# Perceiver block on one core: tile 1's attention and projection ahead of tile 0's FFN, four rotating x buffers, scale rows and half of Wo's low parts on GpSimd

## The reference

```python
# fq(x, s, z) = (clip(round(x / s + z), 0, 255) - z) * s ; ln = layer norm without weights
x = x + fq(ln(x)) @ fq(ctx)                      # x: 16 x 64 x 1024, ctx: 16 x 1024 x 1024
qkv = ln(x) @ Wqkv                               # 32 query heads of 32, one K and one V head
x = x + softmax(q k^T / sqrt(32) + alibi, causal) v @ Wo
routing = softmax(ln(x) @ gate_w.T)              # 8 experts
in_s, out_s = routing @ in_channel_scale, routing @ out_channel_scale
x = x + (ln(x) * in_s) @ sign(W).T * out_s + bias
```

## Time and profile before

| | us |
|---|---|
| median of 3 runs (454.27 to 456.82) | 455.64 |
| the profiled execution's own time | 456.7 |
| its span, first to last instruction | 454.9 |

### The profile page before, as it was taken

The page is one execution under the profiler, slowest core; times in us unless marked ns, Lnnn a source line. Parts: engine busy times, 40 slices in busy tenths (PEclk is TensorE's granted clock), DMA queues, the critical chain, the costliest instruction groups (busy, mean ns, idle before and its releaser), DMA issues.

```text
span 454.9 us, 9598 instructions
## 1 busy us (share of the span) xinstructions
PE 382.6 (84%) x3952; PEld 260.4 (57%) x3952; DVE 313.5 (69%) x584; ACT 258.9 (57%) x308; POOL 99.7 (22%) x112
## 2 busy tenths in 40 slices
PE   0446965996699998999899989998999899889665
PEld 0115844964245874587458845884588458745332
DVE  7688576875737859785978597859885965384331
ACT  4687986564875757565756575657665622242110
POOL 4420010004112312231223122312131212021202
PEclk9999975799599999999999999999999999989759
DMA  7999993599876964596459745974491010001001
GB/s 316 378 410 409 406 408 128 186 343 414 242 276 226 324 215 140 170 339 213 138 164 337 220 140 165 330 226 138 156 339 43 0 48 1 4 0 48 0 0 46
DMA packets 30049, 91.97 MB, mean 202 GB/s; under 512 B 8208, under 2 KB 8208, under 8 KB 29968
## 3 DMA queue, kind: packets, MB, share of 16 engines
q1 hardware_dynamic: 27840, 83.40, 51.5%
q10 hardware_dynamic: 2160, 7.87, 4.6%
HBM read 85.50 MB, written 4.19 MB: 197 GB/s over the span
## 4 chain that ended last, share of the span: by engine, by line
PE 68%; DMA 11%; DVE 10%; ACT 5%; issue 4%; SPq 1%; POOL 1%; POOLq 0%; DVEq 0%; ACTq 0%
DMA ring<-ctx 11%; PE R L1408 11%; PE T L1245 8%; PE R L1198 7%; PE R L1200 7%; PE R L1199 7%; PE R L1278 6%; PE R L1280 6%; PE R L1281 6%; PE C L1226 5%; ACT b L475 4%; PE T L1367 4%; DVE Pr L913 2%; DVE XL L1012 1%; PE R L1302 1%
## 5 line engine op out<-in xcount | busy, mean ns | idle before, releaser
L475 ACT ACTIVATE b<-ring,quant,qpar 128x2048 uint8<-128x2048 f32 x64 | 132.9, 2091 | 11.6 <-DMA ring<-ctx 11.5
L1278 PE MATMUL R<-T_hi,Wqkv_hi 128*128 128x128 f16 x512 | 90.9, 223 | 0.0
L1280 PE MATMUL R<-T_lo,Wqkv_hi 128*128 128x128 f16 x512 | 90.8, 223 | 0.0
L1281 PE MATMUL R<-T_hi,Wqkv_lo 128*128 128x128 f16 x512 | 90.7, 223 | 0.0
L1278 PEld LDWEIGHTS R<-T_hi,Wqkv_hi 128*128 128x128 f16 x512 | 51.8, 101 | 0.4
L1408 PE MATMUL R<-sgn,T_hi 128*128 128x512 fp8e4 x128 | 51.7, 404 | 0.0
L1408 PE MATMUL R<-sgn,T_lo 128*128 128x512 fp8e4 x128 | 51.6, 403 | 0.0
L1280 PEld LDWEIGHTS R<-T_lo,Wqkv_hi 128*128 128x128 f16 x512 | 51.2, 100 | 0.2
L1281 PEld LDWEIGHTS R<-T_hi,Wqkv_lo 128*128 128x128 f16 x512 | 51.2, 100 | 0.0
L1226 PE MATMUL C<-b,aT 128*64 128x512 f16 x256 | 39.6, 439 | 13.5 <-ACT b L475 11.3
L1198 PE MATMUL R<-Wo,attT_hi 128*128 128x512 f16 x128 | 48.6, 380 | 0.4 <-DVE attT_lo L944 0.4
(11 more groups left out here) (131 smaller groups left out, 821.8 us busy)
## 6 DMA issues: line engine op xcount, KB each, us to landing
ring<-ctx SPq DMA_DIRECT2D x64, 1024.0 KB, 5.9
ring<-L_attn_Wo SPq DMA_DIRECT2D x4, 1024.0 KB, 7.5
ring<-L_ffn_weight SPq DMA_DIRECT2D x4, 1024.0 KB, 5.7
out<-X ACTq DMA_DIRECT2D x8, 512.0 KB, 2.6
Wo<-L_attn_Wqkv SPq DMA_DIRECT2D x7, 544.0 KB, 15.5
XN<-x ACTq DMA_DIRECT2D x6, 512.0 KB, 3.4
sgn<-L_attn_Wqkv SPq DMA_DIRECT2D x1, 544.0 KB, 17.5
X<-x ACTq DMA_DIRECT2D x1, 512.0 KB, 3.8
```

Of the source, the lines that this page charges most:

```text
L475: e.activation(b8[:, c % BRING, :], ring[:, slot, :], ACT.Identity, scale=qR2, bias=qZ2).then_inc(s_rf[slot], 1)
L1278: e.matmul(dst, hi, rows[0], start=k == 0 and g == 0, stop=False, skip_group_check=True)
L1280: e.matmul(dst, hi, rows[1], start=False, stop=False, skip_group_check=True)
L1281: last = e.matmul(dst, lo, rows[0], start=False, stop=k == KT - 1, skip_group_check=True)
```

## The change

- Steps 1 and 2 are one list up to tile 2's K and V product. Tile 0's projection goes to PSUM C. The projection is four parts (two output halves n, each in a low and a high half of the contraction). Behind tile 1's queries come the first part for tile 0, tile 1's scores, the other three parts, tile 1's attention and projection among tile 0's second norm, router and tile 2's context products, then tile 0's FFN.
- Four buffers `X0` to `X3` replace `X`, `XN`, `X2`. A tile's x, its sums and its result stay in one buffer.
- The rows scaled for the FFN get their own pair `XS` and no longer share `T16` with the norm's transposes. K's and V's copies are two functions.
- The scale rows are made on GpSimd in step 0, in eight instructions, from a load that now stands behind Wqkv's eight pieces. Their raw rows lie in X2 and X3.
- Of Wo's four low parts, pieces 0 and 2 are made on GpSimd, two instructions each, pieces 1 and 3 stay on VectorE.
- In step 2 the store of tile 0's result stands ahead of the conversions (3, 0) to (3, 2) and of K's and V's copies on ScalarE.

```diff
@@ gpsimd
+            def scales_by_part():
+                e.wait_ge(s_const, 16)
+                e.wait_ge(s_scales, 32)
+                for k in range(2):
+                    part, raw = scales[:, k, :], scales_raw[k]
+                    link(e.tensor_copy(part, raw))
+                    link(e.tensor_tensor(part, part, sign_sb.broadcast_to([4 * E, H]), ALU.mult))
+                    link(e.tensor_tensor(raw, raw, lower_sb.broadcast_to([4 * E, H]), ALU.mult))
+                    last = e.tensor_tensor(part, part, raw, ALU.add)
...
+            def wo_lo(k):
+                e.wait_ge(s_whi, KT + k + 1)
+                hi, lo = (w[:, 2 * k:2 * k + 2, :] for w in Wo)
+                link(e.tensor_scalar(weight_piece(k), weight_piece(k), C_W, None, ALU.mult))
+                e.tensor_tensor(lo, weight_piece(k), hi, ALU.subtract).then_inc(s_rf[k], 1)
...
+            def step_1():
+                subtract_max(e, 0, 0, 1)
+                subtract_max(e, 0, 1, 1)
+                inv_std(1, 1)
+                wo_lo(0)
+                inv_std(0, 2)
+                wo_lo(2)
+                with_row_sum(2)
@@ scalar
             def load_x(t):
-                e.wait_ge(s_xc, t)
-                e.dma_start(XN[:, :], x_v[t]).then_inc(s_x, 16)
+                if t < XBUFS:
+                    e.wait_ge(s_prep, 3)
+                else:
+                    e.wait_ge(s_out, 16 * (t - XBUFS + 1))
+                e.dma_start(X[t % XBUFS][:, :], x_v[t]).then_inc(s_x[t % 2], 16)
...
                 if f:
                     t1_hi(s, 0)
                     t1_hi(s, 1)
+                if s.is_step(2):
+                    store(s)
+                    conv(3, 0)
+                    conv(3, 1)
                 if n:
                     conv(s.i + 1, 2)
                 if f:
-                    kv_copy(s)
+                    k_copy(s)
+                    v_copy(s)
@@ vector, step 1
+                t1_lo(s, 1)
+                wo_lo(1)
                 v_lo(s)
-                ta_lo(s, 0)
                 ta_lo(s, 1)
-                wo_lo(1, 2)
-                k_lo(s)
-                wo_lo(3, 1)
-                q_lo(s, 0)
-                q_lo(s, 1)
                 stats0(2)
                 norm0(2)
+                q_lo(s, 0)
+                k_lo(s)
+                wo_lo(3)
+                q_lo(s, 1)
+                softmax_in(1)
+                softmax_rest(1)
                 x2(s, 0)
@@ tensor, step 1
+                query(s, 1)
+                project(s, 0, low)
+                scores(s, 0)
+                scores(s, 1)
+                project(s, 1, low)
+                project(s, 0, high)
+                pt(ahead, 0, 0)
+                pt(ahead, 0, 1)
+                project(s, 1, high)
+                pv(ahead, 0, 0)
+                pv(ahead, 0, 1)
+                context(2, 0, s)
...
+                context(2, 1)
+                project(ahead, 1, low)
+                context(2, 2)
+                project(ahead, 0, high)
+                context(2, 3)
+                project(ahead, 1, high)
+                outscale(ahead, 0)
+                ffn(ahead, 0, low)
+                outscale(ahead, 1)
+                ffn(ahead, 0, high)
+                t1(ahead)
+                ffn(ahead, 1, low)
+                ffn(ahead, 1, high)
```

538 lines of the change are left out of this document (288 added, 250 removed).

## The result

The changed kernel takes 480.24 us (median of 4 runs, 478.64 to 481.23), the kernel before 456.23 in the same session: a ratio of 1.0531, 95% interval 1.0486 to 1.0576. It is slower, as forecast, but by 24 us, not 17, and 1.2 us above the range. The profiled execution has a span of 476.8 us against 454.9. That is 21.9 us and not 24.0, because the changed kernel's profiled execution was the fastest of its four (478.64) and that of the kernel before (456.7) near its slowest.

What follows compares the result with a forecast made beforehand. TensorE was taken to bound the kernel from 168.1 us, with idle time and low clock before. Terms of 5.6 + 5.3 + 6.5 = +17.4 us gave 474.1 on the profiled execution, 473.0 us as median; range 457 to 479.

Steps and rivals of the forecast that it cites:

- First term: Up to tile 1's K and V product: VectorE's Wqkv low parts wait for GpSimd's scale instructions, +5.6 us.
- Second term: From tile 1's to tile 2's K and V product: GpSimd's Wo pieces hold VectorE, TensorE idles, +5.3 us.
- Of the 4.6 us of low clock I give back 2.0: Between tile 1's and tile 2's K and V products: 2.0 of 4.6 us lost to low clock are recovered.
- Idle: 8.4 + 3.1 + 4.0 = 15.5: Same stretch: TensorE's waits for tile 1's scores, two conversions and remaining conversions, 15.5 us against 8.3 before.
- I take 1.9 for the scaling: GpSimd's scaling, which had no measured row, was priced at 1.9 us, nearest to one stream in.
- my bound of 3.7: Upper price for GpSimd's scaling, from line 416's 3.7 us for 2048 elements.
- for their whole length: VectorE instructions with two SBUF inputs, or quick single-input ones, and GpSimd instructions exclude each other throughout.
- Third term: From tile 2's K and V product to its scores: the store's wait delays K's copy, TensorE idles 6.3 us, +6.5 us.
- the rest: Everything behind tile 2's scores, later steps at 45.6 us each: no change, 0 us.
- Colder still: Rival: gaps of 8.4 and 6.3 us each put TensorE on its low clock, 478 to 481 us; chance 0.08.

Runs made afterwards that it cites:

- e11: The kernel before with only the scale rows changed: loaded behind Wqkv and made in eight GpSimd instructions; 457.19 us, ratio 1.0002.
- e8: The changed kernel with GpSimd's scaling of Wo's pieces written as a product with a broadcast constant; 478.18 us, ratio 1.0492.
- e13: The changed kernel with TensorE's long waits filled with products that nobody reads, nothing moved; 474.54 us, ratio 1.0423.
- e3: The changed kernel with ScalarE's copies of tile 2's K and V ahead of the store and two context conversions; 479.03 us, ratio 1.0507.

## Why the prediction was right, and where it was wrong

**Direction and mechanism: right.** VectorE and GpSimd took turns, the norm of tile 2 was held, TensorE stood idle ahead of the scores, K's copy came 8.8 us late, later steps kept 45.6 us.

**First term, +5.6, measured +3.1.** The low parts were held for 7.0 us (13.47 - 7.29 for six and 0.8 for the seventh, which I left out) where I had 8.2 for five. They began 1.5 us earlier, and the queries ended at 55.7, not 57.7. GpSimd was done at 60.2, not 61.8. In the old order (e11) the same delay was 1.8 us at the product and nothing in the time.

**Second term, +5.3, measured +13.1: the step that failed.** The mechanism was there, and its sizes were wrong. "Of the 4.6 us of low clock I give back 2.0": TensorE was busy for 65.08 us, not 63.05 - 2.0, so 4.0 us off. "Idle: 8.4 + 3.1 + 4.0 = 15.5": it was 19.3, so 3.8 off. Together that is the whole miss of this term, 7.8. Where it arose is seen at the marks.

Up to the scores the forecast held, by luck. Counted from K, the start of tile 1's K and V product, I had them at K + 25.6, and they came at K + 26.0 (108.78 - 82.76). "I take 1.9 for the scaling" was wrong: it took 5.37, beyond even my bound of 3.7. But VectorE's low part 1 ended at K + 4.0, not 6.5, since it ran beside the end of the scaling (see the last section; "for their whole length" doesn't hold there), and its norm met GpSimd's second piece at K + 8.8, not behind 10.7, which took most of that back. TensorE had less to do than I thought and reached the scores at K + 14.8, not 17.2; that makes the wait 11.3 us, not 8.4. The scaling still counts: in e8, 1.77 us less for each brings tile 2's product 1.8 us closer to tile 1's, so by proportion my 1.9 would have been worth some 3.5 us (an estimate).

Behind the scores the rest of the term had 51.0 us, and it took 58.36:

```profile
126.02:167.14 41.12, 36.63 (x196) 20.38 (x197) 16.31 (x34) 19.20 (x19) 5.10 (x6) 0.81 0.57 212
```

The context product began at K + 43.3 (126.02), where I had K + 41.4. The conversions ended at 124.84; the last 1.2 us are the transposing transfer's, which stands behind four loads on SP's queue, and I had not counted that queue. From the product to tile 2's K and V product I had 35.2 us; it took 41.12, 5.9 more, 4.5 of them idle where I had 4.0. The clock behind the product is 0.50 up to 140 us. That is the term's low clock, given back in the forecast and not in the kernel. e13 didn't raise it there, so how much of these 5.9 us a higher clock would return stays open.

**Third term, +6.5, measured +7.9.** Idle 6.07 us against 6.3 forecast; I left the clock out (1.8 us more busy time, 18.94 against 17.15). My cause was incomplete: without the store's wait (e3) the conversions hold the next copy instead.

**The sum.** Its terms are off by -2.5, +7.8 and +1.4, and the rest by -2.2, together 4.5 us in the spans. The other 2.7 us up to 480.24 are the spread of executions: 1.1 taken off for the execution before, and a profiled execution after that was 1.6 under its median.

**Rivals.** "Colder still" has the time (478 to 481) and a chance of 0.08. Its mechanism is half there: at the first of its two gaps e13 takes the low clock away and gains nothing, at the second (the tail) 0.7 us, but the low stretch from 126 us on, behind a wait of 3.5 us, was in no rival of mine. An attention low part, which reads PSUM, wasn't held: in the changed kernel VectorE's line 1005 took its 0.76 us at 87.46, beside GpSimd's subtraction from 86.39 (4.28 us). By the Trainium skill, SBUF — State Buffer, "Who interferes with whom", such an instruction is outside the exclusion; the trace agrees. The range's upper end was drawn from a bound for the scaling that no row of one operand supported.

## What to carry over

An instruction of GpSimd that holds VectorE costs what stands behind the held instruction on VectorE, not its length: the same half of Wo's low parts was free in one order and some 7 us in another. When a list is rewritten, follow each queue, SP's too, to the instruction whose slot it waits for; closing one gap often only uncovers the next releaser. And where TensorE's clock is low behind waits, first see whether the work there is on the path: filling was worth 6 us at the end of the kernel, where it was, and nothing just behind the changed kernel's scores, where it wasn't. Look at the granted clock afterwards, too: where it stayed low, the filling has tested nothing. And a mark that comes at the forecast time (the scores, K + 26.0) doesn't clear the terms that lead to it; two of them were wrong and cancelled.
